# Pacing the indirect scatters by half-scores, and splitting one expert product around z's transpose

## The reference

```python
h = tok(x, ...)                                   # [16, 221, 128], f32
h = h + attn(layernorm(h), w_qkv, w_agg, b_agg)   # 8 heads of 16, softmax over 221 keys
h = h + ffn(layernorm(h), expert_weights, expert_indices, w1, w2)
# ffn: 8 experts, top 2, for 1024 tokens only (T = 1024, x_flat has 3536 rows):
#   sort the 2048 assignments by expert, gather the tokens,
#   y = gelu(xg @ w1[e]) @ w2[e]   (128 -> 512 -> 128), scatter-add w * y to token rows
```

## Time and profile before

| what | us |
|---|---|
| median of 3 runs (258.67 to 259.13) | 259.06 |
| the profiled execution, its own time | 261.23 |
| its span, first to last instruction | 259.4 |
| PE busy | 239.9 |
| DVE busy | 190.4 |
| ACT busy | 138.5 |
| POOL busy | 131.7 |

### The profile page before, as it was taken

How to read it: one execution, slowest core, us unless ns; L and a number is a source line. 1 busy time by engine, 2 the same in 40 slices (tenths; PEclk the granted TensorE clock), 3 DMA queues, 4 the chain that set the end, 5 groups by cost and what they waited for, 6 DMA issues and landing times.

```text
span 259.4 us, 6971 instructions
## 1 busy us (share of the span) xinstructions
PE 239.9 (92%) x2703; PEld 196.5 (76%) x2703; DVE 190.4 (73%) x418; ACT 138.5 (53%) x222; POOL 131.7 (51%) x181
## 2 busy tenths in 40 slices
PE   7999899999999989898699999999989799998994
PEld 6899779667676868686478878787768588886772
DVE  3897746867869787879547686879768597968554
ACT  4870311824343425352255858686857768686460
POOL 7000145231847274747615286475666868685422
PEclk9999999999999999999979999999999999999999
DMA  6999330405565756551614326271625253534422
GB/s 215 412 391 465 138 78 31 105 3 124 162 160 167 166 158 148 178 122 39 144 35 93 77 49 139 39 150 27 144 38 125 55 104 73 92 65 78 80 20 45
DMA packets 30191, 32.00 MB, mean 123 GB/s; under 512 B 3830, under 2 KB 26694, under 8 KB 30128
## 3 DMA queue, kind: packets, MB, share of 16 engines
q1 hardware_dynamic: 25214, 28.17, 38.3%
q0 software_dynamic: 4080, 2.59, 7.7%
q10 hardware_dynamic: 866, 0.81, 1.0%
HBM read 16.24 MB, written 5.95 MB: 86 GB/s over the span
## 4 chain that ended last, share of the span: by engine, by line
PE 58%; DMA 12%; DVE 10%; issue 6%; ACT 6%; POOL 3%; another core or an unknown queue 2%; POOLq 2%; DVEq 0%
PE e_ps L1198 13%; PE s_ps L1198 11%; PE s_ps L1274 10%; DMA out<-y_sb,idx_u 10%; DVE nmax L981 6%; PE m_ps L1386 5%; ACT probs L678 4%; PE m_ps L1259 4%; PE e_ps L1465 3%; PE m_ps L1452 3%; POOL w_now L579 2%; DMA w_raw<-wt 1%; POOLq L575 1%; PE e_ps L1452 1%
## 5 line engine op out<-in xcount | busy, mean ns | idle before, releaser
L981 DVE TENSOR_REDUCE nmax<-s_ps 104x4 fp32r<-104x884 f32 (+1 forms) x60 | 61.8, 1072 | 10.8 <-PE s_ps L1274 10.4
L678 ACT ACTIVATE probs<-s_ps 104x888 f32<-104x888 f32 (+1 forms) x60 | 51.2, 906 | 31.2 <-PE s_ps L1274 26.4
L568 POOL DMA_INDIRECT out<-y_sb,idx_u x23 | 36.4, 1583 | 36.4 <-DMA out<-y_sb,idx_u 28.4
L1274 PE MATMUL s_ps<-pair_a 32*104 32x222 f32 (+1 forms) x504 | 34.5, 307 | 9.1 <-DVE nmax L981 3.8
L1274 PEld LDWEIGHTS s_ps<-pair_a 32*104 32x104 f32 (+1 forms) x504 | 21.2, 169 | 23.7 <-issue 9.8
L498 POOL TENSOR_TENSOR var_eps<-mv,eps_t 128x2 f32<-128x2 f32 x16 | 5.8, 364 | 51.2 <-DVE mv L946 50.5
L531 POOL DMA_INDIRECT z_slots<-z,slot_u x20 | 20.5, 1025 | 15.1 <-PE s_ps L1274 10.6
L1386 PE MATMUL m_ps<-probs,v_aug 104*32 104x221 f32 (+1 forms) x480 | 25.8, 353 | 0.0
L1465 PE MATMUL e_ps<-w_now,hidT 128*128 128x128 f32 x184 | 23.4, 277 | 0.0
L951 DVE TENSOR_SCALAR z_sb<-h_sb,mv,rstd 128x128 f32<-128x128 f32 x32 | 11.1, 388 | 16.7 <-POOL rstd L500 16.7
L1465 PEld LDWEIGHTS e_ps<-w_now,hidT 128*128 128x128 f32 x184 | 21.7, 192 | 0.4 <-POOL w_now L590 0.2
(11 more groups left out here) (164 smaller groups left out, 532.5 us busy)
## 6 DMA issues: line engine op xcount, KB each, us to landing
pair_a<-qk SPq DMA_DIRECT2D x64, 111.0 KB
w_sb<-w SPq DMA_DIRECT2D x8, 512.0 KB
pair_b<-qk SPq DMA_DIRECT2D x30, 111.0 KB
w_raw<-wt SPq DMA_DIRECT2D x6, 512.0 KB, 10.0
x_raw<-x SPq DMA_DIRECT2D x6, 512.0 KB, 9.9
z_slots<-z SPq DMA_DIRECT2D x1, 1518.0 KB, 14.0
zs<-z_slots SPq DMA_DIRECT2D x7, 198.0 KB
x_raw<-x SPq DMA_DIRECT2D x4, 256.0 KB, 4.5
```

Of the source, the lines that this page charges most:

```text
L568: g.indirect_dma_start(rows, bass.IndirectOffsetOnAxis(ap=idx_u[:, at:at + 1], axis=0), y_sb[:, n % 2, i, :], None, compute_op=ALU.add).th ...
L678: s.activation(probs[0:n, blk, 2 * f:2 * f + 2].rearrange("p t u n -> p t (u n)"), s_ps[0:n, 2 * f:2 * f + 2, 0:2 * NE], ACT.Exp, scale=DH ...
L981: v.tensor_reduce(nmax[0:n, blk, 2 * f:2 * f + 2, MAX_ROW[0]:MAX_ROW[1] + 1:2], src, AX_X, ALU.max, negate=True).then_inc(max_ready, 1)
L1274: mm = pe.matmul(dst[0:n, i, u * NE:(u + 1) * NE], a[rs, u, N0 * blk:N0 * blk + n], b[rs, u, :], start=start, stop=stop)
```

## The change

- `zs` becomes two buffers, with a semaphore for each. The load of round 1 is issued behind that of round 0; the load of round n + 2 waits for the transposes, ids and weights of round n, no longer for those of round n + 1.
- On POOL, a cycle of the rounds becomes: `fetch_w2(n)`; after s1's second half scatter 0 of the round before; `fetch_w1` of two tiles; after s2's first half scatter 1; `stage1` (rstd); `fetch_w1` of the third; after s2's second half scatter 2; `keep_h(c+2)`. It was: scatter 0, `keep_h(c+1)`, `fetch_w2(n)`; after s1's second half scatter 1; `fetch_w1` of two; `stage1`; `fetch_w1`; after s2's first half scatter 2.
- In cycle 6 the last four scatters of z's rows wait for s1's second half, s2's first half and s2's second half.
- On PE, `hidden(n+1, 0)` at the end of a cycle does three of its four matmuls; the fourth runs in the next cycle behind `z_turn`. `gelu(n, 0)` on ACT moves behind `o_raw_copy` and `zT_copy`.
- In cycle 7, `zs_turn(0)` moves from ahead of `s1(7, 1)` to behind it; ACT copies its result instead of DVE, and DVE takes ids and weights later in the cycle.

```diff
@@ SP: load_zs
-                if n:
-                    sp.wait_ge(zs_turned, n)
-                    sp.wait_ge(idx_ready, n)
-                    sp.wait_ge(slot_w_ready, n)
-                sp.dma_start(zs[:, 0:ROUND_TILES[n], :],
+                if n == 1:
+                    sp.wait_ge(tok_done, len(UNITS))
+                elif n >= 2:
+                    sp.wait_ge(zs_turned, n - 1)
+                    sp.wait_ge(idx_ready, n - 1)
+                    sp.wait_ge(slot_w_ready, n - 1)
+                sp.dma_start(zs[n % 2][:, 0:ROUND_TILES[n], :],
@@ SP: the loop
-                if n == 0:
-                    load_zs(1)
...
                     load_zs(0)
+                    load_zs(1)
@@ POOL: the loop
-                if n > 0:
-                    scatter_y(n - 1, 0)
-                    if c + 1 < BATCH:
-                        keep_h(c + 1)
                 fetch_w2(n)
                 if 0 <= b < FFN_B:
                     two_rows(b)
                     if paced:
                         first_scores(c, 1)
                     scatter(b, 0, 0)
-                    if paced and b < FFN_B - 1:
+                    if paced:
                         second_scores(c, 0)
                     scatter(b, 0, 1)
                     if b == FFN_B - 1:
                         scatter(b, 1, 0)
-                        scatter(b, 1, 1)
                 if 0 < n <= ROUNDS and paced:
                     first_scores(c, 1)
-                scatter_y(n - 1, 1)
+                scatter_y(n - 1, 0)
                 if n >= 0:
                     fetch_w1(n + 1, 0, 2)
+                if 0 < n <= ROUNDS and paced:
+                    second_scores(c, 0)
+                scatter_y(n - 1, 1)
                 if c + 2 < BATCH:
                     stage1(c + 2)
+                if b == FFN_B - 1:
+                    second_scores(c, 1)
+                    scatter(b, 1, 1)
...
                 if 0 < n <= ROUNDS and paced:
-                    second_scores(c, 0)
+                    second_scores(c, 1)
                 scatter_y(n - 1, 2)
+                if n >= 0 and c + 2 < BATCH:
+                    keep_h(c + 2)
@@ ACT
+            def first_zsT_copy():
+                act.wait_ge(zs_turned, 1)
+                m = ROUND_TILES[0]
+                s.copy(zsT[:, 0:m, :].rearrange("p i s -> p (i s)"), e_ps[:, 0:m * P]).then_inc(zsT_ready, 1)
...
-                if n > 0:
-                    gelu(n, 0)
                 if c - 1 >= 0:
                     o_raw_copy(c - 1)
                 if n > 0 and c + 1 < BATCH:
                     zT_copy(c + 1)
+                if n > 0:
+                    gelu(n, 0)
+                if n == 0:
+                    first_zsT_copy()
@@ DVE: zsT_evac copies zsT only for n > 0; zsT_evac(0) moves behind take_max(7)
@@ PE: hidden
-            def hidden(n, i):
+            def hidden(n, i, c0=0, c1=FC):
...
-                for c in range(FC):
+                for c in range(c0, c1):
...
-                mm.then_inc(hid_done, 1)
+                if c1 == FC:
+                    mm.then_inc(hid_done, 1)
@@ PE: the loop
                 if ahead1 and n > 0:
                     z_turn(c + 1)
-                if n == 0:
-                    zs_turn(0)
+                if n > 0:
+                    hidden(n, 0, FC - 1, FC)
                 tok_some(p0)
                 if here:
                     s1(c, 1)
+                if n == 0:
+                    zs_turn(0)
...
                 if n >= 0:
-                    hidden(n + 1, 0)
+                    hidden(n + 1, 0, 0, FC - 1)
```

More of the change, by code:

```diff
@@ L237, in build @@
         zero = sb("zero", [P, P])
-        zs = sb("zs", [P, ROUND, ROW])
+        zs0 = sb("zs0", [P, ROUND, ROW])
         slot_w = sb("slot_w", [P, N_TILES])
@@ L284, in build @@
         y_sb = sb("y_sb", [P, 2, ROUND, P])
+        zs = (zs0, sb("zs1", [P, ROUND, ROW]))
         nmaxT = sb("nmaxT", [P, NE], F32R)
@@ L360, in build @@
         scattered = [sem(f"scattered{i}") for i in range(2)]
-        zs_in, zs_turned, zsT_ready = sem("zs_in"), sem("zs_turned"), sem("zsT_ready")
+        zs_turned, zsT_ready = sem("zs_turned"), sem("zsT_ready")
+        zs_in = [sem(f"zs_in{i}") for i in range(2)]
         w1_ready, w2_ready, hid_done, hidT_ready = sem("w1_ready"), sem("w2_ready"), sem("hid_done"), sem("hidT_ready")
@@ L442, in load_zs @@
             def load_zs(n):
-                if n:
-                    sp.wait_ge(zs_turned, n)
-                    sp.wait_ge(idx_ready, n)
-                    sp.wait_ge(slot_w_ready, n)
-                sp.dma_start(zs[:, 0:ROUND_TILES[n], :],
+                if n == 1:
[5 more added lines that the diff above has]
+                sp.dma_start(zs[n % 2][:, 0:ROUND_TILES[n], :],
                              z_dram[TILES_BEFORE[n] * P:TILES_BEFORE[n + 1] * P, :].rearrange("(i p) d -> p i d", p=P)
-                             ).then_inc(zs_in, 16)
+                             ).then_inc(zs_in[n % 2], 16)
             for c in range(-1, BATCH + 1):
                 n = c - E0
-                if n == 0:
-                    load_zs(1)
                 if c + 1 < BATCH:
@@ L1082, in zsT_evac @@
                 dve.wait_ge(zs_turned, n + 1)
-                v.tensor_copy(zsT[:, 0:m, :].rearrange("p i s -> p (i s)"), e_ps[:, 0:m * P]).then_inc(zsT_ready, 1)
-                v.tensor_copy(slot_w[:, TILES_BEFORE[n]:TILES_BEFORE[n + 1]], zs[:, 0:m, WEIGHT]).then_inc(slot_w_ready, 1)
-                v.tensor_scalar(idx_u[:, TILES_BEFORE[n]:TILES_BEFORE[n + 1]], zs[:, 0:m, ID], c_sb[:, C_FREE:C_FREE + 1], None,
+                if n:
+                    v.tensor_copy(zsT[:, 0:m, :].rearrange("p i s -> p (i s)"), e_ps[:, 0:m * P]).then_inc(zsT_ready, 1)
+                v.tensor_copy(slot_w[:, TILES_BEFORE[n]:TILES_BEFORE[n + 1]], zs[n % 2][:, 0:m, WEIGHT]).then_inc(slot_w_ready, 1)
+                v.tensor_scalar(idx_u[:, TILES_BEFORE[n]:TILES_BEFORE[n + 1]], zs[n % 2][:, 0:m, ID], c_sb[:, C_FREE:C_FREE + 1], None,
                                 ALU.min).then_inc(idx_ready, 1)
@@ L1118, in _ @@
                     ffn_z(c - 2)
-                if n == 0:
-                    zsT_evac(0)
                 if 0 < n < ROUNDS:
@@ L1137, in _ @@
                     hT_evac(UNIT_ENDS[(c, 0)])
+                if n == 0:
+                    zsT_evac(0)
                 if n >= 0:
@@ L1427, in zs_turn @@
                     return
-                pe.wait_ge(zs_in, 16 * (n + 1))
+                pe.wait_ge(zs_in[n % 2], 16 * (n // 2 + 1))
                 if n:
@@ L1434, in zs_turn @@
                 for i in range(ROUND_TILES[n]):
-                    mm = pe.transpose(e_ps[:, i * P:(i + 1) * P], zs[:, i, 0:P], ident)
+                    mm = pe.transpose(e_ps[:, i * P:(i + 1) * P], zs[n % 2][:, i, 0:P], ident)
                 mm.then_inc(zs_turned, 1)
-            def hidden(n, i):
+            def hidden(n, i, c0=0, c1=FC):
                 if not (0 <= n < ROUNDS and i < ROUND_TILES[n]):
```

## The result

| | us |
|---|---|
| kernel before, median of 4 runs (258.67 to 259.41) | 259.1 |
| changed kernel, median of 4 runs (254.73 to 260.72) | 255.84 |
| ratio, 95% interval | 0.9863 (0.9815 to 0.9911) |
| profiled execution of the changed kernel, its span | 256.33, 254.5 |

Faster by 3.3 us, and 0.1 us from the forecast. The profile does not bear out how the forecast came to it.

The account below looks back on a forecast made before the run. The prediction took the serial chain of three scatters, not PE (92% busy), to set the pace in cycles 10 to 12. Terms -3.3 - 0.2 + 0.3 = -3.2 us gave 255.9 us on the median of 259.06; range 253.0 to 258.9.

Parts of the forecast that it names:

- Step (f): Cycle 6: spacing the last four z_slots scatters priced at 0, between +0.5 and -2 us.
- The loss of 4.03 us in cycles 10 to 13: Cycles 10 to 13 against the 13.11 us of cycles 8 and 9, laid mainly to three serial scatters a cycle.
- Step (b): POOL's new order in the rounds, covering scatter 2's landing; with the moved quarter of hidden -3.3 us in cycles 8 to 13.
- L: Length of a round's chain of three scatter landings and restarts on POOL, forecast as 13.76 us, above PE's 12.89.
- The price of the drift: Chain slower than PE's cycles, so a late rstd starts cycle 14 at 79.4 us after cycle 8's start, against 77.3.
- its sign: Sign that the forecast is right: cycles 8 and 9 each take under 13.0 us.
- Waits for landings: Sign that the forecast is right: POOL's waits for landings in cycles 8 to 13 fall from 16.9 to under 12 us.
- Step (a): Quarter of hidden(n+1, 0) fills PE's hole behind z_turn, 0.22 us a cycle; an undisturbed cycle becomes 12.89 us.
- Step (e): Cycle 7: zs_turn(0) behind s1(7, 1) makes the projection and ACT's exponentials later, +0.3 us.
- The slower one: Rival: scatter 0 slips onto SP's placing of q and k, landings lengthen; 261.1 us, chance 0.13.
- The faster one: Rival: scatter 0 goes ahead of the placing, all landings near 3.4 us, POOL holds nothing; 253.9 us, chance 0.23.
- Given back, 259: Rival: scatter 1's second place behind s2 gives back the first rounds' gain, L about 14.4; 259 us, chance 0.09.

Follow-up runs that it names:

- e1_quarter: The kernel before with only the split hidden (last quarter behind z_turn) and ACT's moved gelu; 259.33 us, ratio 1.0008.
- e2_pool: The kernel before with only POOL's new order of the rounds; 258.64 us, ratio 0.9996.
- e4_no_c6: The changed kernel with cycle 6's four scatters in one row again, without waits; 257.52 us, ratio 0.9982 to the kernel before.
- two chains: The changed kernel with every second scatter_y adding to another tensor, each kind waiting only for its own; output lacks those rows; 252.44 us, ratio 0.9766.
- a_again: The changed kernel, unaltered, measured once more; 255.89 us beside 259.1 of the kernel before, ratio 0.9889.
- e3_c6: The kernel before with only the spacing of cycle 6's last four scatters of z's rows; 257.6 us, ratio 0.9968.
- e9_no_waits: The changed kernel without POOL's waits for the halves of the scores in the rounds; 254.89 us beside 254.34 of the kernel before, ratio 0.9932.
- e11_late_scatter2: The changed kernel with round 0's first scatter at cycle 8's start and each third scatter waiting for the next cycle's s1 first half; 256.56 us, ratio 1.0081.

## Why the prediction came out right

The sum was -3.2 and the measured difference -3.3, from two errors that cancel. That is luck: the gain forecast for the rounds did not come, and one of the same size, priced at 0, came in cycle 6.

- **Step (f) failed.** It took ACT's 4.75 us in cycle 6 "as this execution's own" and priced the spacing at 0, with -2 as the far end. The stall is in all four profiles in which the row stands over the end of s2's first half (4.66 in `e1_quarter`, 4.78 in `e2_pool`, 4.72 in `e4_no_c6`), and 2.30 to 2.35 stand there in the other profiles from chips with late semaphores. Cycles 6 and 7 together gained 3.30 (31.69 to 28.39). The text had the cause in its hand, named it, and decided against it because the profiled execution was 2.2 us above the median.
- **Where those 2.2 us were.** In the rounds. From cycle 8 to the end the profile before took 110.68 us, and nine other profiles with late semaphores (all but the two chains) 107.1 to 108.8, old order or new. The loss of 4.03 us in cycles 10 to 13 that opened the argument was in part this execution's own; its 23 landings took 3.77 us in the mean, those of the nine 3.50 to 3.71.
- **Step (b) failed.** L was forecast as 13.76 and was 13.83 ((232.35 - 163.18) / 5, scatter 0 of cycle 9 to that of cycle 14), but by luck: the first four rounds had 13.4 and the last 15.52; in `a_again` the mean was 13.53. The price of the drift, 2.1 us (79.4 against 77.3) by a late rstd, did not come: DVE waits for rstd nowhere in cycles 8 to 13 (1.5 us in `a_again`). In its place stand 1.3 us of late semaphores (78.60 against 77.3). They also made cycle 9 miss its sign (13.62 for under 13.0). Waits for landings fell to 12.0, just not under 12; PE no longer waits ahead of hidden. But the working put scatter 0 at +3.7 without setting it against the +1.06 (149.78) of before, and it stopped at cycle 14. A serial chain that drifts behind PE's work can also end the kernel: the tail's +2.16 in the profiled execution is in no term (in `a_again` it was +0.08). Alone, the order is worth 0.04% (interval -0.3 to +0.4).
- **Step (a)** was right on its place (12.89 to the hundredth in cycle 8) and worth nothing that can be told alone (0.08% slower, interval -0.3 to +0.5). Which of the other waits took it is not shown; with two chains every cycle has the 12.89.
- **Step (e)** came to its number, +0.32 for +0.3, by another way: in `e4_no_c6`, which has the moved `zs_turn(0)` without the spacing, cycle 7 took 14.66 against 14.72 before, so the move cost nothing. The 0.32 is PE's wait for the slots, which the spacing makes late; (f) had 1.5 us left over there. What the move is for was missed: with the spacing it saves 1.3 us in cycle 7 (16.31 in `e3_c6` against 15.04).
- **The rivals.** The slower one had L = 14.8; the changed kernel's two profiles had 13.83 and 13.53, only `e9_no_waits` (14.3) and `e11_late_scatter2` (14.4) came near. The faster one had L = 12.5, and no profile had it; the shortest landing of all took 3.16 us. "Given back, 259" described in number what the rounds did, though not by its L of 14.4; only cycle 6 kept the kernel from it.

The Trainium skill, "SBUF — State Buffer", section "SBUF: two separate sides", says that PE and ACT never wait on anyone for their ports and that only DVE and GpSimd share a pair. The rows don't speak against it: ACT's exponentials last 1.71 us with a scatter beside them or without. What is late is the signal between engines, of which that section says nothing.

## What to carry to other kernels

Before pricing a stall as one execution's own, look whether another engine does something beside it: here POOL issued four indirect DMAs in a row. A serial chain across many cycles is to be priced from its first link to the kernel's end, since what an order wins between the links is lost again if the first link starts later. And where the profile shows an engine idle behind a matmul that has ended, look for an indirect DMA issued on POOL beside it; placing that DMA just behind the awaited semaphore takes the stall away, if nothing that others need is queued behind it.

## What the runs showed of the hardware

- On two chips, and in the profiles of before and after, a matmul's semaphore can be late while POOL issues an indirect DMA. In the kernel before 50 matmuls with a semaphore ended within 1.25 us after such an issue, and 10 of them were late by 0.31 to 2.44 us, 7.1 us in all; of 179 others none was. In the changed kernel it was 16 of 47 and none of 184. A single scatter delays by up to 0.9 us, the row of cycle 6 by 2.4 to 2.5 in its four profiles. Why most matmuls beside a scatter are not late stays open.
- One chip had none of it in three profiles (161 matmuls beside a scatter), and the kernel before was 4.8 us faster there. The cause of the difference between chips stays open.
- An indirect DMA that adds 64 KB landed in 3.2 to 5.6 us from its issue, mean 3.50 to 3.87 over the 23 of a profile.
